# Softmax maxima laid into the score banks by ScalarE instead of by matmuls, in a one-core Trainium2 kernel of scan, mixer and attention

## The reference, cut to what matters

```python
latent_kv = x @ w_kv_down                  # rank 128
kv = latent_kv @ w_kv_up                   # keys and values of 16 heads
q = (x @ w_q).reshape(B, T, 16, 64)
att = einsum('bqhd,bkhd->bhqk', q, k) * 64 ** -0.5
att = where(causal, att, -inf)
att = softmax(att, axis=-1)                # exp(att - row maximum) / sum
y = einsum('bhqk,bkhd->bqhd', att, v).reshape(B, T, 1024)
return y @ w_out
```

## Time and profile before

| | |
|---|---|
| time, median of 3 runs | 2116.74 us (2111.61 to 2118.76) |
| profiled execution, first to last instruction | 2113.7 us |
| granted TensorE clock, mean | 0.980 |
| instructions in the profile | 35206 |
| first score matmul of attention | at 288.3 us |
| start of the first unit of the second period | at 422.3 us |

### The profile page before, as it was taken

One profiled execution on the slowest core, in us unless ns is written; L12 is line 12 of the kernel. 1 busy time (PEld: TensorE's weight loads), 2 busy tenths in 40 slices (PEclk: granted clock), 3 DMA queues, 4 the chain that ended last, 5 costly groups with the idle time before them and its releaser, 6 DMA issues.

```text
span 2113.7 us, 35206 instructions
## 1 busy us (share of the span) xinstructions
PE 1984.7 (94%) x12886; PEld 1240.9 (59%) x12886; DVE 1337.2 (63%) x2728; ACT 1097.9 (52%) x2236; POOL 1425.9 (67%) x812
## 2 busy tenths in 40 slices
PE   8997788999999999999989999999999999999898
PEld 6775454555655555555555655555555555555466
DVE  7786555576656666666665657576756575656443
ACT  5775543455545454545455444545445445444585
POOL 1333225778687878787857687868786878687822
PEclk9998899999999999999999999999999999999999
DMA  3000000000000000000000000000000000000001
GB/s 124 1 1 1 0 7 13 13 19 10 13 18 16 13 19 12 19 10 19 13 12 17 12 20 11 17 12 20 11 18 11 20 11 18 11 14 11 26 26 60
DMA packets 29243, 37.01 MB, mean 18 GB/s; under 512 B 6928, under 2 KB 20368, under 8 KB 29072
## 3 DMA queue, kind: packets, MB, share of 16 engines
q1 hardware_dynamic: 29072, 34.76, 5.4%
HBM read 30.02 MB, written 4.46 MB: 16 GB/s over the span
## 4 chain that ended last, share of the span: by engine, by line
PE 63%; DVE 14%; POOL 12%; ACT 6%; issue 4%; DMA 1%; POOLq 0%; ACTq 0%; SPq 0%; DVEq 0%
PE heads_out L918 16%; POOL acc L1416 10%; PE beside L723 9%; PE scores L723 7%; PE two_heads L874 7%; PE scores L897 4%; PE scores L903 4%; PE scores L899 4%; PE scores L901 4%; DVE part_max L1112 3%; ACT prob L1331 2%; PE two_heads L723 2%; PE beside L929 2%; PE heads_out L723 1%; DVE wQK_lo L1073 1%
## 5 line engine op out<-in xcount | busy, mean ns | idle before, releaser
L1416 POOL TENSOR_TENSOR acc<-acc,prob 128x1024 f32<-128x1024 f32 (+3 forms) x512 | 1017.9, 1988 | 195.4 <-ACT prob L1331 140.1
L1331 ACT ACTIVATE prob<-scores 128x512 f32<-128x512 f32 (+3 forms) x1280 | 579.4, 539 | 649.2 <-PE scores L903 289.0
L1112 DVE TENSOR_REDUCE part_max<-two_heads 128x2 f32<-128x1024 f32 x384 | 469.3, 1222 | 280.5 <-PE two_heads L874 279.7
L918 PE MATMUL heads_out<-prob,V 128*64 128x512 f32 (+3 forms) x2560 | 544.4, 547 | 0.0
L1109 DVE CUSTOM_DVE_ANT_0 two_heads<-two_heads,mask 128x128 f32<-128x128 f32 (+3 forms) x512 | 242.0, 514 | 180.4 <-PE two_heads L874 180.4
L874 PE MATMUL two_heads<-k_hi,q_hi 64*128 64x512 f32 (+3 forms) x1280 | 274.1, 424 | 62.8 <-DVE part_max L1112 30.6
L918 PEld LDWEIGHTS heads_out<-prob,V 128*64 128x64 f32 x2560 | 156.7, 137 | 232.4 <-issue 209.6
L874 PEld LDWEIGHTS two_heads<-k_hi,q_hi 64*128 64x128 f32 x1280 | 120.6, 184 | 256.6 <-issue 133.4
L897 PE MATMUL scores<-q_hi,k_hi 64*128 64x512 f32 (+3 forms) x1280 | 236.1, 364 | 0.8 <-DVE k_lo L1100 0.5
L903 PE MATMUL scores<-neg_max,sel 64*128 64x512 f32 (+3 forms) x1280 | 235.6, 362 | 0.0
L901 PE MATMUL scores<-q_lo,k_hi 64*128 64x512 f32 (+3 forms) x1280 | 235.5, 362 | 0.0
(11 more groups left out here) (301 smaller groups left out, 2898.7 us busy)
## 6 DMA issues: line engine op xcount, KB each, us to landing
rden<-rden_rows SPq DMA_DIRECT2D x128, 128.0 KB, 2.9
X<-u SPq DMA_DIRECT2D x8, 512.0 KB, 8.7
out<-X SPq DMA_DIRECT2D x8, 512.0 KB, 2.9
wQK_raw<-wQuery SPq DMA_DIRECT2D x16, 192.0 KB, 3.1
wO_raw<-wOut SPq DMA_DIRECT2D x16, 128.0 KB, 2.8
wV_raw<-wValue SPq DMA_DIRECT2D x8, 128.0 KB, 2.9
den<-den_rows SPq DMA_DIRECT2D x64, 4.0 KB
rden_rows<-den SPq DMA_DIRECT2D x64, 4.0 KB, 1.3
```

What stands on the lines that cost most here:

```text
L918: made = pe.matmul(heads_out[head(h), x0:], V[vn % NVS][:, tt, p % 2, head(h)], prob[step % NPROB][:, h, x0:], start=t == 0, stop=t == TPB ...
L1112: made = ve.reduce_max(part_max[:, t, :, c:c + 1], two_heads[:, :, 0:width], AX.X)
L1331: ac.activation(prob[step % NPROB][:, h, x0:], bank(task, h)[:, x0:], ACT.Exp).then_inc(empty(task, h)[0], 1)
L1416: po.tensor_tensor(total[:, :, x0:], total[:, :, x0:], new[:, :, x0:], ALU.add).then_inc(acc_ok, 1)
```

## The change

1. turn_max, `sel`, `neg_max` and the fourth product go. Each score bank pair is first written by ACT with minus the maxima (**seed**, one ACTIVATE of up to 1024 columns from SBUF to PSUM), and the three products add to it (`start=False`). In four seeds, whose banks were last used in another way, PE first runs two dummy products (`opened`).
2. The maxima reach ACT as a tile `top`, the same 1024 values on all 128 partitions. minus_max now also transposes its column on DVE in 32x32 squares; **rows_out** sends the rows to DRAM with four DMAs of 8x32 values; **spread_max** reads them back onto all partitions with one DMA (512 KB written). There are two `top` tiles. Both are on SP's queue.
3. The planner puts the seeds of the next two steps behind the fillers of a round, ahead of weigh and of the tasks for finished units. rows_out comes a round after minus_max, spread_max three rounds after that, or at the latest ahead of the unit's first seed.
4. Exp takes both heads in one ACTIVATE of up to 1024 columns.
5. In units with j of 2 or 3 DVE sums the first two prob tiles, by a tensor_reduce over two interleaved tiles (prob and acc now lie in one tensor, `sums`); POOL starts with the third. In shorter units POOL does all as before.

The core of the diff:

```diff
@@ Plan.add
+        elif kind == "seed":
+            _, idx, t = task
+            n = 2 * (self.step_of[idx, t] % 2)
+            self.seed_free[idx, t] = sorted({self.freed[b] for b in (n, n + 1) if self.freed[b]})
+            if not (self.whole[n] and self.whole[n + 1]):
+                self.opened[idx, t] = len(self.opened) + 1
...
@@ Plan.need
+        elif kind == "spread_max":
+            idx = task[1]
+            assert ("minus_max", idx) in self.done and self.unseeded(idx - NMAX)
+            self.need("rows_out", idx)
+            if idx:
+                self.need("spread_max", idx - 1)
+        elif kind == "seed":
+            self.need("spread_max", task[1])
         elif kind == "score":
-            self.need("turn_max", task[1])
+            self.need("seed", *task[1:])
...
@@ Plan.attention
             if idx is not None:
-                fillers.append((s + 2, self.start[idx] - 4, ("turn_max", idx)))
+                spreads.append((s + 2, "rows_out", idx))
...
+            if self.layers_done:
+                for step in steps[s + 2:s + 4]:
+                    self.need("seed", *step)
+            for at, kind, idx in spreads[:]:
+                if at <= s and (kind == "rows_out" or self.unseeded(idx - NMAX)):
+                    spreads.remove((at, kind, idx))
+                    self.need(kind, idx)
+                    if kind == "rows_out":
+                        spreads.append((s + 6, "spread_max", idx))
...
@@ tensor_program, score
+                    w.wait_ge(seeded, plan.seeds[idx, t][0])
...
-                    for h in range(2):
-                        pe.matmul(bank(task, h)[:, x0:], sel[head(h), :], neg_max[idx % NMAX][head(h), x0:], start=False, stop=True).then_inc(full(task, h)[0], 1)
+                    for n, (k, q) in enumerate(terms((k_hi[g], k_lo[g]), (q_hi[i], q_lo[i]))):
+                        for h in range(2):
+                            made = pe.matmul(scores[:, first + h, x0:], k[head(h), kc], q[head(h), x0:], start=False, stop=n == 2, skip_group_check=True)
+                    made.then_inc(full(task)[0], 1)
...
@@ vector_program
+                    w.wait_ge(row_max_ok, idx + 1)
+                    ve.transpose(rows[:, idx % 2, :], row_max[:, :]).then_inc(rows_ok, 1)
+                elif kind == "accumulate" and task[2] == 1 and plan.dve_begins(task[1]):
+                    _, idx, t = task
+                    step = step_of[idx, t]
+                    a, z = (SUMS.index(("prob", x % NPROB)) for x in (step - 1, step))
+                    w.wait_ge(*empty(("score", idx, t)))
...
+                    both = sums[:, a:z + 1:z - a, :, :].rearrange("p k h x -> p (h x) k")
+                    ve.tensor_reduce(acc[idx % 2].rearrange("p h x -> p (h x)"), both, AX.X, ALU.add).then_inc(acc_begun, 1)
...
@@ scalar_program
+                elif kind == "seed":
+                    _, idx, t = task
+                    x0 = P * max(0, t - TPB * UNITS[idx][2])
+                    first = 2 * (step_of[idx, t] % 2)
+                    w.wait_ge(*top_here(idx))
...
+                    ac.activation(scores[:, first:first + 2, x0:], top[idx % NMAX][:, :, x0:], ACT.Copy, scale=-1.0).then_inc(seeded, 1)
...
-                        ac.activation(prob[step % NPROB][:, h, x0:], bank(task, h)[:, x0:], ACT.Exp).then_inc(empty(task, h)[0], 1)
+                    ac.activation(prob[step % NPROB][:, :, x0:], scores[:, first:first + 2, x0:], ACT.Exp).then_inc(empty(task)[0], 1)
...
@@ gpsimd_program, accumulate
-                    if t == 0:
+                    if t == 0 or t == 1 and plan.dve_begins(idx):
                         continue
...
@@ sync_program
+                elif kind == "rows_out":
+                    idx = task[1]
+                    w.wait_ge(rows_ok, idx + 1)
+                    if idx >= NTOP:
+                        w.wait_ge(*top_here(idx - NTOP))
+                    for n in range(0, P, SQ):
+                        sp.dma_start(top_rows[idx % NTOP, :].rearrange("(a x) -> a x", x=P)[:, n:n + SQ],
+                                     rows[n:n + 2 * TPB, idx % 2, :]).then_inc(top_out[idx % 2], 16)
+                elif kind == "spread_max":
+                    idx = task[1]
+                    w.wait_ge(top_out[idx % 2], 64 * (idx // 2 + 1))
+                    if idx >= NMAX:
+                        w.wait_ge(seeded, plan.seeds[last_step(idx - NMAX)][0])
+                    sp.dma_start(top[idx % NMAX].rearrange("p h x -> p (h x)"), top_rows[idx % NTOP:idx % NTOP + 1, :].broadcast_to([P, 2 * BLK])).then_inc(top_in[idx % 2], 16)
```

More of the change, by code:

```diff
@@ L722, in product @@
                 for n, (l, r) in enumerate(pairs):
-                    made = pe.matmul(dst, l, r, start=first and n == 0, stop=last and n == len(pairs) - 1)
+                    made = pe.matmul(dst, l, r, start=first and n == 0, stop=last and n == len(pairs) - 1, skip_group_check=not first)
                 return made
@@ L939, in tensor_program @@
                         cs = slice((2 * half + q) * P, (2 * half + q + 1) * P)
[L940 removed]
+                        made = product(bank(task)[:, q * C:(q + 1) * C], terms((oT_hi[:, cs], oT_lo[:, cs]), (wO_hi[n % 2][:, :], wO_lo[n % 2][:, :])), first=q == 0)
                     made.then_inc(full(task)[0], 1)
```

181 lines of the change are left out of this document (92 added, 89 removed).

## The result

The changed kernel takes 2328.8 us (median of 4 runs, 2325.0 to 2338.0), the kernel before 2115.3 in the runs beside it: a ratio of 1.101, with a 95% interval of 1.098 to 1.104. The direction is the one forecast; the loss is 214 us where about 100 were forecast, and 2329 lies above the range.

The account below looks back on a forecast made before the run. PE was taken as the bound, with POOL close behind in the two long units. +6.2 us a period times 15 = 93, plus 10 in the first period, on 2113.7 gave 2217, stated as 2215; range 2150 to 2270.

Parts of the forecast that it names:

- the late spread: Round 5: the third unit's spread, issued at about 4.4 us behind the inversion, lands at 8.0; TensorE waits, +5.0 us.
- POOL's late start in U3: Round 13: POOL's first own addition waits for DVE's sum and starts at 7.1 us instead of 2.39.
- three signs of being wrong: Seeds of U2 find their tile there, seeds cost well over 1 us, or attention's mean round falls below 5 us.
- That makes round 6 wait another 1.1 us less its gain of 0.5, and a bit of slack: +0.4.: Round 6: second seed and oT_hi queue behind the stalled seed on ACT, delaying POOL and project; +0.4 us.
- So plain seeds are hidden: Ordinary rounds: ACT's seeds let the next score start at 3.85 us, below round 5's 4.04; rounds 0 to 4 gain 0.6.
- the wait that the forecast named and sized too small: Round 12: project arrives at +1.75 us and waits 1.9 us for POOL's late oT_lo; the round +1.5 us.
- Rounds 13 to 19 ... given back there: 0.: PE's savings, 3.2 us of products and 1.2 of turns, are given back as POOL runs 2.0 us late; net 0.
- the first period, +10 forecast: First period: unit 2's stores and spread come about 8 us late, unit 1's about 4, other rounds return 2; +10 us.
- (1): Rival: PE stays the bound and every wait is hidden, 1950 us, faster; chance 0.10.
- (2): Rival: the spread is late but POOL's delay is absorbed by the acc and prob buffers, 2045 us, faster; chance 0.10.
- (3): Rival: both costs at half, no change or a little slower, 2100 to 2150 us; chance 0.07.
- (4): Rival: POOL blocks DVE's sum like two-input operations, up to 2.4 us more at 30 places, 2290 us; chance 0.11.

Follow-up runs that it names:

- the run with the transposes: The changed kernel with 44 transposes of 128 columns on TensorE ahead of the wait for the third unit's first seed, 14 times; 2322.0 us, ratio 1.100.

## Why the prediction was wrong

The account of the loss, from the kernel before to the changed one, by the medians of the runs (the steps add up to 215 us): the rows in place of the turns -18, the seeds in place of the product +118, DVE's sums +17 (+25 alone), the late spread +98; the merged Exp 0. By rounds, in us a period, forecast and measured:

```
rounds            0 to 4     5      6     7 to 12   13 to 19    sum
forecast           -0.6    +5.0   +0.4     +1.4        0       +6.2
measured           +0.1    +5.2   +2.4     +2.3      +2.0     +12.0
```

**What held.** The late spread: +5.0 forecast for round 5, +5.2 measured. It came by the path forecast: issued at 3.9 us after the start (4.4 forecast), landing in 4.0 (3.6), the seed done at 9.0 (9.0). That the end is met is in part luck: the issue came 0.5 us sooner than forecast, and the landing took 0.4 longer. The 3.6 was a median over two unlike groups, eight loads of X at 8.7 us and eight stores at 2.9. The estimate from the Trainium skill's figures (DMA: Bandwidth & Descriptors, "Anatomy of one DMA"), 3.2 us, would have been further off. POOL's late start in U3: 7.1 us forecast, 7.5 measured. The seed, the merged Exp, the sum on DVE: within 4% each. A round as short as ACT allows, 3.85 us: round 10 is 3.8, and 3.6 with short seeds (round 19, at 3.9, is as it was before). None of the three signs of being wrong came: the seeds of U2 did not find their tile, a seed takes 1.03 us, and attention's mean round is 5.9 us. They could not tell this loss from the forecast one. One reading is off without effect: round 12 started 27.83 us after round 7, not 27.75.

**The step that failed first: "That makes round 6 wait another 1.1 us less its gain of 0.5, and a bit of slack: +0.4."** It was +2.4. Two things were left out. Project has its second half in bank 0, so the seeds of round 7 wait for DVE's addition, and their own 1.0 us each comes behind that. With the early spread, where round 5 has no stall, round 6 is still +1.5. The second is the clock, forecast nowhere: 0.66 in that round of the sample period, and on average 1.0 us of it (the run with the transposes).

**The step behind it: "So plain seeds are hidden".** It counted from the first score product to the next first one, in a round with nothing else in bank 0: 3.85 us. It held for such rounds alone. Where bank 0 is used (6, 7, 8, 9, 12, 15, 18) the two seeds come behind the work in that bank. And the second step's products wait for the second seed, 0.94 us behind the first, so that a pair of steps saves 0.13 us where I had 0.46. I had that arithmetic for rounds 7 and 9 and let it stand for two rounds; round 8 has it too (+0.8, forecast +0.4). The run with short seeds shows that it is their length, 92 us: it brings rounds 6 and 8 back and takes rounds 0 to 4, forecast at -0.6 and measured at +0.1, to -1.6. Round 12 (+2.3, forecast +1.5) is another matter: of that, short seeds take back 0.5, and the rest is POOL's oT_lo, the wait that the forecast named and sized too small. Round 15 (+1.2, forecast 0) is 6.0 us in five of the seven periods, as it was before in four of these; two periods at 8.1 and 10.8 us, with the granted clock at 0.79 and 0.68, make the mean, and their cause was not tried.

**The third: "Rounds 13 to 19 ... given back there: 0."** It was +2.0. The forecast had POOL 2.0 us late at the end of its row and TensorE 4.4 us ahead, and set the two against each other without a row for it. POOL's delay is absorbed only in part by its gaps, as I said; but project of U2 in round 18 is where it comes due, as oT_lo starts 2.1 us into that round in the trace, with the seeds behind project's bank. In three of the seven periods the clock comes on top: round 18 is 9.1 to 11.2 us long with 0.81 to 0.70 granted, against 6.5 to 7.5 at 1.00. Rounds 16 and 17 gave 1.4 back, round 18 took 2.2. With the sums on POOL round 18 is 6.5.

**The fourth: the first period, +10 forecast, +23.8 measured.** The rows' lateness, which was all that I costed, is 3.4 by the run without seeds; DVE's sums are 2.6; the other 17.8 go with the seeds. Short seeds take back only 4.4 of the 23.8, so it is mostly not their length. That it is their place, in rounds full of keys, queries and splits for ACT, is likely but not shown.

The rivals: (1) and (2), with the waits hidden, are refuted by the rounds. (3) didn't occur. What (4) assumed does not happen to this sum, but it does to subtractions with two inputs in SBUF (last section). The case that came true, that both costs have company, was not among them: the forecast had each unit's stall end where its cause ended.

What stays open: the seeds cost 118 us net, and cutting them short took 92 off (measured beside DVE's sums, not without). How the rest divides between the place in ACT's order, POOL's lateness in round 12, and the clock was not tried apart.

## What to carry to other kernels

Work that is moved to an idle engine is not free when that engine works in order and stands between two others: ACT was busy 52%, and a microsecond of seeds between Exp and the next products cost 118 us net over 640 steps. So cost such a move in every round, by what shares the bank and what is queued behind, not in the shortest one; and when the parts are separable, keep the part that removes work for nothing (the turns, -18 us) and put the rest only where nothing waits behind it (-14 us more). A stall of TensorE is to be priced with what follows it, since the clock may fall behind it, and matmuls then start nearly twice as far apart (0.43 us for 0.23 here).

## What the runs showed of the hardware that was not expected

- The clock fell behind a wait of 1.64 us, too. The changed kernel in round 12: the matmul that ends the wait, from the timeline.

```profile
1488.92 0.48 PE L767 MATMUL beside<-wO_hi,oT_hi 128*128 128x256 f32 x1 [1.64 <-POOL oT_lo L1473]
```

  And windows of 1 us around it; TensorE had been busy in 3.33 of the 3.71 us of round 11 and for the first 2 us of round 12:

```profile
1486.30:1487.30 1.00, 0.98 (x8) 0.41 (x6) 0.42 (x1) 1.00 (x2) 1.00 (x1) 1.00 0.03 3
1487.30:1488.30 1.00, 0.00 (x0) 0.00 (x0) 0.98 (x1) 0.72 (x2) 1.00 (x2) 1.00 0.00 0
1488.30:1489.30 1.00, 0.38 (x2) 0.38 (x3) 0.24 (x1) 0.45 (x1) 1.00 (x2) 0.88 0.00 0
1489.30:1490.30 1.00, 1.00 (x7) 1.00 (x7) 0.00 (x0) 0.00 (x0) 0.86 (x2) 0.50 0.00 0
...
1492.30:1493.30 1.00, 1.00 (x10) 0.43 (x6) 0.17 (x1) 0.73 (x1) 0.00 (x0) 0.91 0.00 0
```

- Copying 1024 columns from SBUF to PSUM takes ACT 1026 ns, Exp of as many from PSUM to SBUF 1022; at 512 columns it is 607 and 597. With both sides in SBUF 512 columns take 620 (oT_hi, written as fp32r).
- The 512 KB spread to 128 partitions lands after 4.0 us, 1.1 later than rden's 128 KB.
- A subtraction on DVE with both inputs in SBUF waits for the addition that POOL has under way. wO_lo, 256 columns, took 1.64 us in the run with seeds in five rounds; in the run without seeds it is

```profile
1350.50 0.96 DVE L1137 TENSOR_TENSOR wO_lo<-wO_raw,wO_hi 128x256 fp32r<-128x256 f32 x1 [0.96 <-ACT wO_hi L1336]
```

  What differs is how much of POOL's running addition was left when it started: 1.35 us in the one, 0.68 in the other, and in both it ended 0.28 us behind the addition's end. So it did in all 200 cases in the fourteen traces here, with lengths from 0.5 to 2.6 us; where POOL was idle it took 0.42 us. The tensor_reduce of the run with DVE's sums alone was not held up by POOL's oT_lo in that way.
